# Gate and up weights are prepared in turns beside the first FFN steps

## The reference

```python
gate = jnp.einsum('bsd,hd->bsh', x, w_gate)          # hidden 2048
up = jnp.einsum('bsd,hd->bsh', x, w_up)
ffn = jnp.einsum('bsh,dh->bsd', silu(gate) * up, w_down)

x = x + 0.5 * ffn(layernorm(x))
x = x + attention(layernorm(x), w_qkv, w_out, q_gain)   # causal, rotary on every other head
x = x + 0.5 * ffn(layernorm(x))
```

## Time and profile before

| | before |
|---|---|
| median of 3 runs | 2766.74 us (2766.33 to 2767.2) |
| the profiled execution, its own time | 2768.96 us |
| its span | 2765.7 us |
| PE busy | 2695.6 us (97%) |
| DVE busy | 1789.2 us (65%) |
| ACT busy | 1178.4 us (43%) |

### The profile page before, as it was taken

How to read it: one execution, slowest core, us unless ns; L and a number is a source line. 1 busy time by engine, 2 the same in 40 slices (tenths; PEclk the granted TensorE clock), 3 DMA queues, 4 the chain that set the end, 5 groups by cost and what they waited for, 6 DMA issues and landing times.

```text
span 2765.7 us, 55193 instructions
## 1 busy us (share of the span) xinstructions
PE 2695.6 (97%) x22208; PEld 1961.6 (71%) x22208; DVE 1789.2 (65%) x5118; ACT 1178.4 (43%) x2186; POOL 526.3 (19%) x820
## 2 busy tenths in 40 slices
PE   4999999999999999999999999999999999999999
PEld 4677766776777777777767777677777766776676
DVE  7766766676766665666656666566666766676643
ACT  5443544354434443343434444344443445354422
POOL 0012132213131301203021120312103131313100
PEclk8999999999999999999999999999999999999999
DMA  7000000000000000000000000000000000000000
GB/s 260 1 16 9 17 9 1 9 17 24 1 9 16 24 1 3 7 17 24 2 3 16 8 24 1 5 21 18 7 9 17 16 9 1 9 17 16 2 9 16
DMA packets 51391, 47.71 MB, mean 17 GB/s; under 512 B 36288, under 2 KB 36288, under 8 KB 50624
## 3 DMA queue, kind: packets, MB, share of 16 engines
q1 hardware_dynamic: 51136, 44.19, 5.1%
HBM read 26.35 MB, written 9.44 MB: 13 GB/s over the span
## 4 chain that ended last, share of the span: by engine, by line
PE 87%; DVE 8%; issue 3%; ACT 2%; POOL 1%; DMA 0%; SPq 0%; DVEq 0%; ACTq 0%
PE psum L1064 26%; PE psum L1066 26%; PE psum L1065 26%; PE psum L1219 2%; PE psum L1195 2%; PE psum L1231 2%; PE psum L1087 1%; DVE arena L900 1%; DVE arena L902 1%; ACT arena L792 1%; PE psum L1232 1%; DVE arena L895 1%; PE psum L1177 1%; DVE arena L979 1%; DVE ss L841 0%
## 5 line engine op out<-in xcount | busy, mean ns | idle before, releaser
L1064 PE MATMUL psum<-arena,WG 128*128 128x256 f16 x2048 | 558.9, 273 | 4.9 <-DVE arena L902 3.4
L1064 PE MATMUL psum<-arena,WU 128*128 128x256 f16 x2048 | 558.7, 273 | 0.0
L1066 PE MATMUL psum<-arena,WG 128*128 128x256 f16 x2048 | 558.6, 273 | 0.0
L1065 PE MATMUL psum<-arena,WG 128*128 128x256 f16 x2048 | 558.5, 273 | 0.0
L1066 PE MATMUL psum<-arena,WU 128*128 128x256 f16 x2048 | 558.5, 273 | 0.0
L1065 PE MATMUL psum<-arena,WU 128*128 128x256 f16 x2048 | 558.4, 273 | 0.0
L900 DVE SCALAR_TENSOR_TENSOR arena<-arena,psum 128x256 f32<-128x256 f32 x512 | 215.1, 420 | 446.9 <-ACT arena L792 443.4
L792 ACT ACTIVATE arena<-psum,tscale 128x256 f32<-128x256 f32 x512 | 241.4, 472 | 577.7 <-PE psum L1066 576.9
L1064 PE MATMUL psum<-WD,arena 128*128 128x512 f16 x1024 | 388.3, 379 | 3.9 <-DVE arena L906 3.9
L1066 PE MATMUL psum<-WD,arena 128*128 128x512 f16 x1024 | 387.9, 379 | 0.0
L1065 PE MATMUL psum<-WD,arena 128*128 128x512 f16 x1024 | 387.9, 379 | 0.0
(11 more groups left out here) (143 smaller groups left out, 4363.7 us busy)
## 6 DMA issues: line engine op xcount, KB each, us to landing
arena<-in_L_attn_x SPq DMA_DIRECT2D x16, 512.0 KB, 3.6
arena<-arena SPq DMA_DIRECT2D x128, 64.0 KB, 2.1
out<-arena SPq DMA_DIRECT2D x16, 512.0 KB, 2.8
arena<-in_L_ffn_w_gate SPq DMA_DIRECT2D x4, 1024.0 KB, 9.2
arena<-in_L_ffn_w_up SPq DMA_DIRECT2D x4, 1024.0 KB, 6.7
WD<-in_L_ffn_w_down SPq DMA_DIRECT2D x4, 1024.0 KB, 11.4
arena<-in_L_attn_w_qkv SPq DMA_DIRECT2D x1, 3072.0 KB, 21.4
arena<-in_L_attn_w_out SPq DMA_DIRECT2D x1, 1024.0 KB, 5.1
```

Source lines behind the costliest of these rows:

```text
L1064: T_.matmul(o, lhs(0), rhs(0), start=first, stop=False)
L1065: T_.matmul(o, lhs(0), rhs(1), start=False, stop=False)
L1066: return T_.matmul(o, lhs(1), rhs(0), start=False, stop=last)
```

## The change

The kernel does the same arithmetic with the same products. What is changed is mostly the order:

- **Tiles in turns.** Tiles alternate between gate and up (j even is gate), so that tiles 0 and 1 hold what the FFN steps 0 to 3 need, 2 and 3 steps 4 to 7, and so on. Tiles 0 and 1 are prepared ahead of piece 0, with the layer norm of the first two token tiles between them. Tiles 2 to 7 are prepared beside pieces 0 to 23, one tile per four pieces. Gate and up pieces wait for their tile's low parts (`w_lo`) where j is a multiple of 4.
- **Smaller stages.** Tile 0 is loaded and scaled in two halves. The scaling of the rows is signalled per half tile, turn and parts per PSUM bank; five banks are used in turns. One of four small DVE instructions per tile goes, since the reciprocal gives the scale directly (even tiles have one more instead, L893, for `tscale`).
- **Places in SBUF.** `RAW` lies where the down weights will be, `RAWD` at the end of the arena and in `xb`; tokens of the first layer norm go through the space of `WQ`.
- **SP's order.** First the tiles, then tokens and down weights between them, then the rotary table and the gains. The load of `w_qkv` and `w_out` waits until `w_down` is turned.
- **What follows is shifted.** "wd turn" moves from pieces 1 to 16 to pieces 24 to 29 (three per piece), "wd parts" from pieces 20 to 35 to pieces 32 to 46, the maximum of a block of `w_down` is taken in four instructions. The preparation of the gains moves from the start to piece 48. "magnitude" is taken in sixteen instructions from piece 40 on, sent over the partitions at piece 56 and used at piece 61. "weights" is done in sixteen blocks at pieces 62 to 77, "pickers" at 76 to 82.
- **Shares.** Four entries of `FEW` and `MANY` are changed. Attention starts at piece 82 as before.

```diff
@@ order(): the start
-        put(("w scales", 0), ("w rows", 0), ("w scales", 1))
-        for j in range(8):
-            if j + 2 < 8:
-                put(("w scales", j + 2))
-            if j + 1 < 8:
-                put(("w rows", j + 1))
-            put(("w turn", j))
-            if j == 7:
-                put(("stats", 0, 0, 0), ("stats", 0, 0, 1), ("norm", 0, 0, 0), ("turn", 0, 0, 0), ("norm", 0, 0, 1))
-            put(("w out", j))
-        put(("split", 0, 0, 0), ("turn", 0, 0, 1), ("split", 0, 0, 1))
-        normalize(24, 0, 0, (2, 3))
-        late = {n + 1: [("wd turn", n), ("wd out", n)] + [("wd max", n // 4)] * (n % 4 == 3) for n in range(HC)}
-        late[19] = [("wd scales", 0)]
-        for k in range(HC):
-            late[20 + k] = [("wd parts", k)]
-        late.update({37 + 2 * k: [("magnitude", 0, k)] for k in range(KC)})
-        late.update({45: [("magnitude", 1, 0)], 47: [("scales", 0, 0)], 50: [("weights", 1, 0)]})
-        late.update({53 + 2 * g: [("pickers", g)] for g in range(GH)})
-        late.update({52 + 4 * k: [("weights", 0, k)] for k in range(KC)})
+        put(("w scales", 0), ("w rows", 0, 0), ("w rows", 0, 1), *turns(0, 0, 1, 2, 3), ("w scales", 1))
+        put(("stats", 0, 0, 0), *parts_of(0, 0, 1), ("stats", 0, 0, 1), ("w rows", 1, 0), ("w rows", 1, 1), *parts_of(0, 2, 3))
+        put(("norm", 0, 0, 0), ("norm", 0, 0, 1), *turns(1, 0, 1), ("turn", 0, 0, 0), ("split", 0, 0, 0), *turns(1, 2, 3))
+        put(*parts_of(1, 0, 1), ("turn", 0, 0, 1), ("split", 0, 0, 1), *parts_of(1, 2, 3), ("w scales", 2))
+        late = {n: [] for n in range(100)}
+        for i in range(3):
+            a, b, n = 2 * i + 2, 2 * i + 3, 8 * i
+            m = n + (i == 0)
+            late[n] += [("w rows", a, 0)]
+            late[n + 1] += [("w rows", a, 1), ("w scales", b)]
+            late[m + 2] += turns(a, 0, 1)
+            late[m + 3] += turns(a, 2, 3) + parts_of(a, 0, 1)
+            late[m + 4] += parts_of(a, 2, 3)
+            late[n + 4] += [("w rows", b, 0)]
+            late[n + 5] += [("w rows", b, 1)] + [("w scales", a + 2)] * (i < 2)
+            late[n + 6] += turns(b, 0, 1)
+            late[n + 7] += turns(b, 2, 3) + parts_of(b, 0, 1)
+            late[n + 8] += parts_of(b, 2, 3)
+        for m in range(HC):
+            late[24 + m // 3] += [("wd turn", m), ("wd out", m)]
+            late[25 + m // 3] += [("wd max", m // 4, i) for i in range(4) if m % 4 == 3]
+        late[31] += [("wd scales", 0)]
 ...
@@ shares
-            "head": 1, "end": 1, "end values": 0.5, "out 0": 1, "out 1": 2, "out 2": 1.5, "out 3": 1,
+            "head": 1, "end": 0.8, "end values": 0.5, "out 0": 2, "out 1": 2, "out 2": 1.5, "out 3": 1,
 ...
@@ sync
+            for j in range(8):
+                w = (w_up if j % 2 else w_gate)[j // 2 * 512:(j // 2 + 1) * 512, :].rearrange("(i p) d -> p i d", p=P)
+                if j >= 4:
+                    sp.wait_ge(s["w_tr"], 4 * (j - 3))
+                if j == 0:
+                    for i in (0, 2):
+                        sp.dma_start(RAW[0][:, i:i + 2, :], w[:, i:i + 2, :]).then_inc(s["raw0" if i == 0 else "half0"], 16)
+                else:
+                    sp.dma_start(RAW[j % 4], w).then_inc(s[f"raw{j % 4}"], 16)
+                if j == 1:
+                    token_half(0)
 ...
+            sp.wait_ge(s["dn_tr"], HC)
             sp.dma_start(RAWQ, w_qkv.rearrange("(k p) n -> p k n", p=P)).then_inc(s["qkv_in"], 16)
@@ scalar
+            def scale_rows(j, half):
+                act.wait_ge(s["wsent"], j + 2 if j else 1 + half)
+                for i in (2 * half, 2 * half + 1):
+                    r = RAW[j % 4][:, i, :]
+                    ins = nc.scalar.activation(r, r, ACT.Copy, scale=wscale[:, w_stats(j, i, 1)])
                 ins.then_inc(s["wscaled"], 1)
@@ vector
+                    link(V_.tensor_reduce(wmax[:, c], rows, AX_X, ALU.max, apply_absolute_value=True))
+                    link(V_.tensor_scalar(wpow[:, c], wmax[:, c], LEAST, 2.0 ** -13, ALU.max, ALU.mult))
+                    link(V_.tensor_scalar(wpow[:, c].bitcast(I32), wpow[:, c].bitcast(I32), EXP_BITS, None, ALU.bitwise_and))
+                    V_.reciprocal(wscale[:, c], wpow[:, c]).then_inc(s["wsent"], 1)
@@ tensor
+            def w_turn(j, k):
+                if k == 0:
+                    pe.wait_ge(s["wscaled"], 2 * (j + 1))
+                if 4 * j + k >= 5:
+                    pe.wait_ge(s["w_lo"], 4 * j + k - 4)
+                for i in range(4):
+                    ins = T_.transpose(ps(w_bank(j, k), i * P, P), RAW[j % 4][:, i, k * P:(k + 1) * P], ident[:, :])
+                ins.then_inc(s["w_tr"], 1)
 ...
@@ tensor, gate(j) and up(j)
+                if j < HC and j % 4 == 0:
+                    pe.wait_ge(s["w_lo"], 2 * j + 4)
 ...
+                if j < HC and j % 4 == 0:
+                    pe.wait_ge(s["w_lo"], 2 * j + 8)
```

More of the change, by code:

```diff
@@ L83, in build @@
     xn = [words("xn"), words("qt", 0, D)]
+    xn += [WQ.rearrange("p s k n -> p (s k n)").bitcast(F32)[:, i * D:(i + 1) * D] for i in range(2)]
     XT = [halves(n).rearrange("p (s k n) -> p s k n", s=2, k=KC) for n in ("xt", "xt2")]
@@ L128, in build @@
     RAWQ = arena[:, at - KC * 3 * D:at].rearrange("p (k n) -> p k n", k=KC)
-    WDflat = WD.rearrange("p s k n -> p (s k n)").bitcast(F32)
-    RAWD = [WDflat[:, HID * i:HID * (i + 1)] for i in range(4)]
+    RAWD = [words("xb")] + [arena[:, at - HID * i:at - HID * (i - 1)] for i in (3, 2, 1)]
     RAWO = words("xb")
@@ L455, in order, with turns, parts_of @@
-        late.update({52 + 4 * k: [("weights", 0, k)] for k in range(KC)})
+        def turns(j, *chunks):
+            return [("w turn", j, k) for k in chunks]
+        def parts_of(j, *chunks):
+            return [("w out", j, k) for k in chunks]
+        put(("w scales", 0), ("w rows", 0, 0), ("w rows", 0, 1), *turns(0, 0, 1, 2, 3), ("w scales", 1))
+        put(("stats", 0, 0, 0), *parts_of(0, 0, 1), ("stats", 0, 0, 1), ("w rows", 1, 0), ("w rows", 1, 1), *parts_of(0, 2, 3))
+        put(("norm", 0, 0, 0), ("norm", 0, 0, 1), *turns(1, 0, 1), ("turn", 0, 0, 0), ("split", 0, 0, 0), *turns(1, 2, 3))
@@ new lines, in order @@
+        for m in range(HC):
+            late[24 + m // 3] += [("wd turn", m), ("wd out", m)]
+            late[25 + m // 3] += [("wd max", m // 4, i) for i in range(4) if m % 4 == 3]
+        late[31] += [("wd scales", 0)]
+        for k in range(HC):
+            late[32 + k - (k > 0)] += [("wd parts", k)]
+        normalize(WHEN, 0, 0, (2, 3))
+        late[48] += [("gains",)]
+        for n in range(HC):
+            late[40 + n] += [("magnitude", n)]
+        late[56] += [("maxima sent",)]
@@ L456, in order @@
+        late[61] += [("scales",)]
+        for n in range(HC):
+            late[62 + n] += [("weights", n)]
+        for g in range(GH):
+            late[76 + 2 * g] += [("pickers", g)]
+        put(*late[0])
         while ("split", 0, 1, 1) not in seen or at[0] < first_piece[2, 0, HC] - 12:
@@ L478, in order @@
         return o
+    WHEN = 34
     LOAD, LEFT, PACE = 9, 3, (0, 2, 3, 4)
@@ L483, in build @@
             "maxima": 1, "max rows": 1, "scores": 1, "exp": 1.5, "high": 1, "low": 1, "max": 1,
-            "head": 1, "end": 1, "end values": 0.5, "out 0": 1, "out 1": 2, "out 2": 1.5, "out 3": 1,
+            "head": 1, "end": 0.8, "end values": 0.5, "out 0": 2, "out 1": 2, "out 2": 1.5, "out 3": 1,
             "dup": 3}
-    FEW = {"qk": 1, "qk first": 2, "ends": 2.4, "stack": 2, "v first": 1.5, "turned": 1, "max first": 0.32,
-           "maxima": 1, "max rows": 0.8, "scores": 0.8, "exp": 1.2, "high": 0.8, "low": 0.8, "max": 0.56,
+    FEW = {"qk": 1, "qk first": 2, "ends": 2.4, "stack": 2, "v first": 2.25, "turned": 1, "max first": 0.32,
+           "maxima": 1, "max rows": 0.8, "scores": 0.8, "exp": 1.2, "high": 0.56, "low": 0.8, "max": 0.56,
            "head": 0.56, "end": 0.8, "end values": 1, "out 0": 1.25, "out 1": 1.25, "out 2": 1, "out 3": 1.5,
@@ L494, in xn_of @@
     def xn_of(b, u, t):
+        if (b, u) == (0, 0) and t < 2:
+            return 2 + t
         return t % 2 if (b, u) in ((0, 0), (B - 1, 2)) else 0
```

174 lines of the change are left out of this document (89 added, 85 removed).

## The result

| | before | after |
|---|---|---|
| median of 4 runs | 2766.64 us (2766.33 to 2767.2) | 2739.41 us (2739.15 to 2739.88) |
| ratio | | 0.9899 (95% interval 0.9885 to 0.9913) |
| span of the profiled execution | 2765.7 us | 2737.3 us |
| PE busy | 2695.6 us | 2689.7 us |

The account below looks back on a forecast made before the run. The prediction took the start to be bound by DVE and everything later by PE. Gate 16 23.1 us earlier, 1.5 behind it and 0 for shares made 24.6 us less: a median of 2742 us, range 2735 to 2751.

Parts of the forecast that it names:

- What bounds: Whole run: the start is bound by DVE behind the first load, everything later by PE.
- Until the first gate: Start, tiles 0 and 1: DVE is the queue; gate 0 starts at 22 us, range 21 to 24.5.
- Tiles 2 to 7: Beside pieces 0 to 23: a loop through DVE and ACT takes 8.5 us a tile.
- w_down: Turning and splitting the down weights: down 0 starts at 95.5 us after PE stands about 3 us.
- case D: Rival beside tiles 2 to 7: PE keeps the low clock, 34 us more, 2776 us; chance 0.03.
- Downs: Downs 0 to 13: 18.2 us plus 0.9 for two turns of tokens, DVE closely keeping up; gate 16 at 114.8.
- Behind gate 16: From 138 to 160 us before: 1.5 of PE's 2.8 us standing is given back, bounds 0 and 2.8.
- Shares: Attention, four changed table entries: worth 0, bounds 4 us either way.
- The sum: Whole run: 23.1 + 1.5 = 24.6 us less, a median of 2742 us.
- A: Rival beside the tiles: dearer ACT and DVE handshakes, 10.3 us a tile, 7 us more, 2749 us; chance 0.17.
- B: Rival at the downs: fed too slowly, about 1.7 us each, 5.6 us more, 2748 us; chance 0.12.
- C: Rival, more gain: tiles at 7.8 us, down 0 hardly waits, tables help by 2; 2735 us; chance 0.13.

Follow-up runs that it names:

- e5: Changed kernel with both halves of the row scaling of tiles 3 to 7 in front of the odd step's tanh on ACT; 2744.5 us.
- e3: Changed kernel with DVE using the maxima of the projections at piece 57 instead of 61; 2747.0 us.
- e4: Changed kernel with the layer norm of the second half's tokens from piece 24 on instead of 34; 2739.7 us.
- e9: Changed kernel with 32 unused identity transposes on PE behind up 15, in the wait for down 0; 2739.3 us.
- e6: Changed kernel with tiles 2 to 7 prepared ahead of piece 0, as before the change; 2765.0 us.
- f2: Changed kernel with the second half's layer norm from piece 37 instead of 34, plus 32 unused transposes behind up 15; 2736.3 us.
- f1: Changed kernel with the layer norm of the second half's tokens from piece 37 on instead of 34; 2737.8 us.
- f3: f2 with all row scalings of tiles 3 to 7 behind the odd step's tanh on ACT; 2734.7 us.
- e7: Changed kernel with the share "high" of FEW back at 0.8, the other new shares kept; 2742.5 us.

## Why the prediction was right, point by point

- **What bounds.** Right. PE's idle time in the spans fell by 22.5 us (70.1 to 47.6) and its busy time by 5.9 (2695.6 to 2689.7), with the same instructions: less of them ran at the low clock, which before lies in the first 66 us.
- **Until the first gate.** Right: 22.4 for 22. The chain of DVE held step by step (second split at 21.53 for 20.8, tile 1's last part at 23.3 for 23).
- **Tiles 2 to 7.** The loop was right and e5 confirmed it; its size was 7.8 to 8.0 us a tile and not 8.5. I had summed durations where start to start counts: two row scalings take 1.23 and not 1.3, the tanh behind them 0.35 and not 0.5, an even step's DVE work overlaps. First gate to gate 12 took 50.8 us for 53 forecast.
- **w_down.** Down 0 at 93.6 for 95.5, from the same loop; the wait in front of it 4.1 for 3. That this wait would take the clock down was missed. My case D had looked for the low level beside the tiles; in this kernel it came behind the one long wait, for 3.4 us, and cost 1.3. In e3 and e4 PE had the low level beside the first tiles as well, from about 16 to 26 us, and the first gate (22.4 and 22.6) and gate 12 (73.2 and 73.4) stand within 0.2 us of where they stand in the kernel after: DVE had the scales of two tiles to do meanwhile, so the clock was not what closed the loop there.
- **Downs.** This step failed in two ways. (Its own sum, 95.5 + 18.2 + 0.9, is 114.6 and not 114.8.) It counted 14 downs; between down 0 and gate 16 stand 15, since down 14 is put in front of gate 16: 19.43 us of the kernel before are 15 x 1.30, which I could have seen there, and I left the surplus unexplained. That is 1.3 us. And it let POOL's rstd follow its input at once: 1.4 us of PE idle, DVE 3.8. Gate 16 came at 117.2 for 114.8, 20.7 earlier and not 23.1.
- **Behind gate 16.** The stall of 2.8 us is regained in full, where I took 1.5: gate 19 is 23.5 us earlier.
- **Shares.** I took 0 with bounds of 4; they gave 5.0 to 5.4 us, outside the bounds. The reason given (stages move by one or two pieces only) was no bound at all: the waits were under 1.1 us each, so a move by one piece of 1.3 us is enough to remove one.
- **The sum.** 20.7 + 2.8 = 23.5 from the start, of which 23.2 stands at attention, and 5.2 from the shares: 28.4 (27.2 by the medians). I had 23.1 + 1.5 + 0 = 24.6. The number was close by luck, because misses cancelled: downs 1.3, clock 1.3 and POOL 1.4 too good, tiles 1.9, the stall 1.3 and the shares 5 too bad.
- **Rivals.** A, tiles of 10.3 us: no. B, downs fed too slowly: partly, 1.57 us each in the mean (turns included) instead of 1.30, but by POOL and the clock; DVE's maxima of 512 columns follow each other in 0.59 us. The formula that the prediction takes there from the Trainium skill, VectorE: DVE Perf Modes, is stated for adds of two tensors, and four reduces of 512 columns in a row took 2.37 us here, not 2.76. C had the right sign and nearly the right size, but only partly by its own terms: the tables helped, by 5 us where it had 2, and tiles took 7.8 to 8.0 us where it had 7.8, but PE waited longer for down 0, not less. D: no.

## What to carry to other kernels

Once work is moved beside a bound engine, read where each of its queues closes a loop, in start-to-start times, and move only what stands in front of the closing instruction: two activations more in front of it cost 5.0 us, two less gained 1.7. A wait has three prices: itself, what stands behind it in the same queue, and, on PE, the clock afterwards; where two losses stand in a row, removing the first may show nothing, since the second takes it back: the two together gave 3.1 us, the first alone 0.1 and the second alone 1.6. And many short waits of PE are worth a try with the tables that space the work, even where a profile shows hardly a single one above a microsecond.

## What was not expected of the hardware

POOL changes between its reduction over the partitions and ordinary instructions with a delay that the profile calls issue. From an ordinary instruction's end to the reduction it was 5.7 us (after), 6.0 (e3) and 6.1 (e4, e9), each time with the input waiting; from the reduction's end to the next ordinary instruction 10.7 (after), 11.2 (e6, e9), 10.8 (e5, f2), 11.0 (f1), 10.6 (f3) and 10.4 us (e7), also with the input waiting. In the kernel before the same change took place unseen: the reduction ended at 96.38, the next input came 10.0 us later, and rstd began at 106.53, 10.1 us behind the reduction. No run shows what POOL does in that time.

In the kernel after PE's granted clock stayed at 1.00 through 70 us in which PE was busy 86% with waits of up to 2.4 us, and fell to 0.50 behind a wait of 4.1 us, for 3.4 us. In e9 it fell behind a wait of 2.7 us, also for 3.4 us. Behind the wait of 6.4 us in e3, and one of 3.9 us in e4, it was 6.8 us long, and so it was in e6 behind the same wait of 4.1 us for down 0; so the length of the wait does not set how long the low level lasts. And the same work in the same order does not always get the same level: e3 differs from the kernel after only from piece 57 on, and yet has this row at 18 to 26 us, where the kernel after runs its first gate at 22.36 with matmuls of 0.27 us, the duration at the full clock.

```profile
18.00:26.00 8.00, 6.50 (x32) 0.50 1.05 406
```
